# The end of a second attention layer reordered, its loads issued one per step, and 24 products on constants put in front of a mixture of experts

## The reference, cut to what matters

```python
q = (Q @ w_q.T); k = (K @ w_k.T); v = (V @ w_v.T)
attn = softmax(where(causal, einsum('bnghd,bmgd->bnghm', q, k) / sqrt(8), -inf))
x = x + tanh(g_xattn[1]) * (einsum('bnghm,bmgd->bnghd', attn, v).reshape(B, S, D) @ w_o.T + b_o)

z = layernorm(x); logits = z @ w_gate            # 2048 tokens, 8 experts, top 1
mask1 = one_hot(argmax(softmax(logits)), 8)
locations1 = cumsum(mask1, axis=0) - mask1       # place in the expert's queue, capacity 256
mask1 = mask1 * (locations1 < 256)
x = x + tanh(g_ffn[1]) * combine(gelu(dispatched @ w1) @ w2)
```

## Time and profile before

| | before |
|---|---|
| median of 3 executions | 1349.39 us (1348.5 to 1352.16) |
| the profiled execution, its own time | 1351.38 us |
| its span, first to last instruction | 1349.6 us |
| mean granted clock of TensorE | 0.98 of full speed |
| busy: TensorE, VectorE, ScalarE, GpSimd | 93%, 81%, 70%, 52% |
| attention 1: first raw scores to the last residual | from 1031.5 to 1226.7 us of the span |
| experts: first to last product | from 1246.6 to 1343.8 us |

### The profile page before, as it was taken

How to read it: one execution, slowest core, us unless ns; L and a number is a source line. 1 busy time by engine, 2 the same in 40 slices (tenths; PEclk the granted TensorE clock), 3 DMA queues, 4 the chain that set the end, 5 groups by cost and what they waited for, 6 DMA issues and landing times.

```text
span 1349.6 us, 28140 instructions
## 1 busy us (share of the span) xinstructions
PE 1253.2 (93%) x10492; PEld 1091.1 (81%) x10492; DVE 1092.6 (81%) x2203; ACT 946.8 (70%) x2153; POOL 705.6 (52%) x618
## 2 busy tenths in 40 slices
PE   1688999999999999999999999979999999995998
PEld 1577999999999999999999999866776454454998
DVE  8979889999989999989999999986434778765554
ACT  5799877778887778887788887645122466572775
POOL 5657555565665566655655554442000356563575
PEclk9889999999999999999999999999999999996999
DMA  4222332222123222133221010024544324217662
GB/s 146 87 62 69 99 95 87 76 71 65 54 78 88 76 69 68 52 79 89 65 70 35 26 36 24 23 68 140 64 75 72 67 42 74 60 45 242 214 231 80
DMA packets 117574, 110.05 MB, mean 82 GB/s; under 512 B 12187, under 2 KB 101499, under 8 KB 117312
## 3 DMA queue, kind: packets, MB, share of 16 engines
q1 hardware_dynamic: 114320, 99.03, 27.5%
q0 software_dynamic: 2944, 9.19, 1.9%
q10 hardware_dynamic: 176, 0.04, 0.0%
HBM read 80.20 MB, written 28.07 MB: 80 GB/s over the span
## 4 chain that ended last, share of the span: by engine, by line
PE 77%; DVE 14%; issue 3%; ACT 2%; DMA 2%; POOL 1%; POOLq 0%; SPq 0%; ACTq 0%; DVEq 0%
PE PC L577 8%; PE SS L543 7%; PE PO L559 7%; PE B L521 5%; PE PA L479 4%; PE PA L481 4%; PE B L1224 3%; PE PO L1208 2%; PE B L1734 2%; PE SS L535 2%; PE PA L492 2%; PE PA L491 2%; PE PA L493 2%; PE SS L2276 2%; PE PA L504 2%
## 5 line engine op out<-in xcount | busy, mean ns | idle before, releaser
L1021 POOL TENSOR_TENSOR RB<-YS,M 128x512 bf16<-128x512 f32 x128 | 161.3, 1260 | 279.4 <-DVE YS L860 279.4
L665 ACT ACTIVATE QT<-B,sm 128x256 f32<-128x256 f32 x256 | 131.3, 566 | 142.2 <-PE B L521 141.7
L479 PE MATMUL PA<-WH,XQ 128*128 128x256 f32 x512 | 141.0, 307 | 17.9 <-DVE WL L808 13.3
L1016 POOL TENSOR_TENSOR yy<-vv,half 128x14 f32<-128x14 f32 (+1 forms) x64 | 147.6, 2306 | 5.3
L543 PE MATMUL SS<-QT,KT 128*128 128x256 f32 x512 | 133.1, 382 | 7.8 <-DVE mx L812 7.6
L481 PE MATMUL PA<-WL,XQ 128*128 128x256 f32 x512 | 130.1, 286 | 0.0
L824 DVE TENSOR_REDUCE vv<-SQ 128x7 f32<-128x896 f32 (+1 forms) x128 | 120.7, 943 | 0.3 <-ACT SQ L711 0.3
L479 PEld LDWEIGHTS PA<-WH,XQ 128*128 128x128 f32 x512 | 98.9, 193 | 19.1 <-DVE WL L808 13.7
L832 DVE TENSOR_TENSOR QN<-QN,yy 128x512 f32<-128x512 f32 x128 | 114.0, 891 | 0.0
L812 DVE TENSOR_REDUCE mx<-SS 128x4 bf16<-128x512 f32 x128 | 88.0, 687 | 26.2 <-PE SS L535 25.2
L521 PE MATMUL B<-identf,QN 128*128 128x128 f32 x768 | 105.7, 274 | 2.0 <-ACT LNT L620 1.1
(11 more groups left out here) (359 smaller groups left out, 4120.6 us busy)
## 6 DMA issues: line engine op xcount, KB each, us to landing
W<-in_w SPq DMA_DIRECT2D x16, 1024.0 KB
XK<-xk_d SPq DMA_DIRECT2D x24, 512.0 KB, 4.3
V<-v_d SPq DMA_DIRECT2D x112, 64.0 KB
v_d<-VST SPq DMA_DIRECT2D x48, 128.0 KB, 2.0
Q<-qsc SPq DMA_DIRECT2D x48, 128.0 KB
WR<-in_wprojT SPq DMA_DIRECT2D x16, 256.0 KB, 3.0
xk_d<-XK SPq DMA_DIRECT2D x8, 512.0 KB, 3.9
kt_d<-KT SPq DMA_DIRECT2D x64, 64.0 KB, 1.6
```

Source lines behind the costliest of these rows:

```text
L479: pe.matmul(PA[:, 256 * k:256 * k + 256], XQ[:, k, c, bs], wh[:, c, 256 * k:256 * k + 256], start=c == 0, stop=False)
L665: a.activation(QT[i % 2][:, o:o + 256], B1[:, o:o + 256], ACT.Identity, bias=col(n + "b"), scale=col(n + "w"))
L1016: p.tensor_tensor(yy[j % 2][:, :, 0:n], v_, half[:, 0:2 * n].rearrange("p (h k) -> p h k", h=2), ALU.pow).then_inc(s_rstd, 1)
L1021: p.tensor_tensor(RB[i % 2][:], YS[:], M[:], ALU.subtract).then_inc(s_rb, 1)
```

## The change

It has three parts. In attention 1 the 12 loads of the last quarter of queries are issued one per step (steps 33 to 44), each behind a wait for TensorE's progress (`sp_pace`), and the stores of the rows are paced alike and spread over more steps. In the tail the roots are taken block by block (12, 13, 14, 15 apart), the next turns, logits and scales of blocks 8 to 13 come earlier, the choice for the first set stands in step 72 before the normalisation of the last units, and some PSUM banks are exchanged for that; the choice and the address arithmetic have fewer VectorE operations, and the loads of the second and later experts wait for the first gather. Ahead of the first expert TensorE makes 8, 12 and 4 products of a 128x128 identity with 512 columns of ones, into a bank that nobody reads before it is overwritten.

```diff
-        next_bs = [range(0, 4), range(4, 8), range(8, 12), range(12, 15), range(15, 16)]
-        NEXT = {32: 0, 48: 1, 64: 2}
-        LAST = N1 + 11
+        next_bs = [range(0, 4), range(4, 8), range(8, 12), range(12, 13), range(13, 14), range(14, 15), range(15, 16)]
+        NEXT = {32: 0, 48: 1, 63: 2, 67: 3, 71: 4}
+        LAST = N1 + 10
...
+        def sp_pace(sp, n):
+            sp.wait_ge(*((s_S, N + n) if n <= N1 else (s_ST, N + n - 8)))
+        def sp_last_queries(sp, i):
+            half, z = divmod(i, NP)
+            if i == 0:
+                sp.wait_ge(s_qst[3], 32)
+            src = qsc[QPART[z]].rearrange("(a h d) t -> h d a t", h=2, d=8)[half]
+            r0 = 64 * half + 8 * z
+            sp.dma_start(Q6[r0:r0 + 8, 3, :, :], src[:, :, 1536:2048]).then_inc(s_qg[3], 16)
...
-                    if b in (2, 3, 7, 8):
-                        sp_queries(sp, 2 + b // 7, b in (3, 8))
+                    if b in (2, 3):
+                        sp_queries(sp, 2, b - 2)
+                if 33 <= n < 45:
+                    sp_pace(sp, n)
+                    sp_last_queries(sp, n - 33)
...
-                    if 0 <= n - 12 * k - 42 < 12:
-                        sp_next_row(sp, 4 * k + (n - 12 * k - 42) // 3, (n - 12 * k - 42) % 3)
+                    if 0 <= n - 12 * k - 45 < 12:
+                        sp_pace(sp, n)
+                        sp_next_row(sp, 4 * k + (n - 12 * k - 45) // 3, (n - 12 * k - 45) % 3)
+                for p in range(2 * (n - 66), 2 * (n - 66) + 2):
+                    if 0 <= p < 12:
+                        sp_next_row(sp, 8 + p // 3, p % 3)
             sp_load_w(sp, 0)
-            for k in range(2, 5):
-                sp_next_rows(sp, k)
+            for b in range(12, NB):
+                for part in range(3):
+                    sp_next_row(sp, b, part)
...
# pe_attention_1
+                if n == 73:
+                    pe_next_turn(pe, 13)
+                if n == 72:
+                    pe_turn_1(pe, 30)
...
-                if 72 <= n < 76:
-                    pe_logits(pe, n - 64)
+                if 68 <= n < 72:
+                    pe_logits(pe, n - 60)
...
-                if 70 <= n < 74:
-                    pe_next_turn(pe, n - 62)
+                if 66 <= n < 70 or n == 71:
+                    pe_next_turn(pe, n - 58 - (n == 71))
-            pe_logits(pe, 11)
             pe_turn_1(pe, 31)
+            pe_out_proj(pe, 14)
+            pe_logits(pe, 12)
+            pe_out_turn(pe, 15)
+            pe_logits(pe, 13)
             pe_queue_places(pe, 0)
-            pe_out_turn(pe, 15)
             pe_out_proj(pe, 15)
-            for b in (12, 13, 14):
+            for b in (14, 15):
                 pe_next_turn(pe, b)
-            for b in (12, 13, 14):
                 pe_logits(pe, b)
-            pe_next_turn(pe, 15)
-            pe_logits(pe, 15)
...
# dve_attention_1
-                if 67 <= n < 71:
-                    dve_next_scale(v, 2, (n - 59,))
-            dve_logits(v, 10)
-            dve_logits(v, 11)
-            dve_choose(v, 0)
+                if 65 <= n < 69:
+                    dve_next_scale(v, 2, (n - 57,))
+                if n == 69:
+                    dve_next_scale(v, 3, next_bs[3])
+                if n == 72:
+                    dve_next_scale(v, 4, next_bs[4])
+                    dve_logits_quad(v, 2)
+                    dve_choose(v, 0)
+                if n == 73:
+                    dve_normalise(v, 30)
+            dve_normalise(v, 31)
             dve_residual_1(v, 14)
             dve_next_stats(v, 14)
-            dve_next_root(v, 3)
-            dve_normalise(v, 31)
-            dve_next_scale(v, 3, next_bs[3])
+            dve_next_root(v, 5)
             dve_queue_places(v, 0)
+            dve_next_scale(v, 5, next_bs[5])
+            dve_compare(v, range(0, 2))
             dve_residual_1(v, 15)
             dve_next_stats(v, 15)
-            dve_next_root(v, 4)
-            dve_compare(v, range(0, 4))
-            dve_next_scale(v, 4, next_bs[4])
-            dve_compare(v, range(4, 12))
-            for b in range(NB - 4, NB):
-                dve_logits(v, b)
+            dve_next_root(v, 6)
+            dve_compare(v, range(2, 5))
+            dve_next_scale(v, 6, next_bs[6])
+            dve_compare(v, range(5, 12))
+            dve_logits_quad(v, 3)
...
# experts
-        locs = B2[:, 0:128]
+        locs = POa[:, 0:128]
-        who = (B1[:, 0:3 * E], PC[:, 0:3 * E])
+        who = (B1[:, 0:3 * E], B1[:, 3 * E:6 * E])
...
         def sp_experts(sp):
             after_attention_1(sp)
+            sp.wait_ge(s_d[0], 32)
             for x_ in range(1, E):
                 sp_load_w(sp, x_)
...
+        def pe_keep_clock(pe, n):
+            for _ in range(n):
+                pe.matmul(SS[:], identb[:], onesb[:].unsqueeze(1).broadcast_to([128, 4, 128]), start=True, stop=True)
...
             pe_who(pe, 1)
+            pe_keep_clock(pe, 8)
             pe_weights(pe)
+            pe_keep_clock(pe, 12)
             pe_tokens_turn(pe, 0)
+            pe_keep_clock(pe, 4)
...
# dve_choose: the comparison reads the logits themselves; the subtraction moves behind the choice
             v.tensor_reduce(mx, lg, AX, ALU.max).then_inc(*vs.up())
             v.wait_ge(*vs.at())
+            v.tensor_tensor(oh, lg, bc(mx, n), ALU.is_equal).then_inc(*vs.up())
...
-            v.tensor_scalar(oh, lg, 0.0, None, ALU.is_equal).then_inc(*vs.up())
...
# dve_routing: both halves of an expert's list in one operation
-            for z in range(2):
-                w = who[z]
-                v.tensor_copy(TU[:, :, z], w[:, E:2 * E]).then_inc(*vs.up())
-                v.wait_ge(*vs.at())
-                v.scalar_tensor_tensor(out=TI[:, :, z], in0=w[:, 0:E], scalar=128.0, in1=TU[:, :, z], op0=ALU.mult,
-                                       op1=ALU.add).then_inc(*vs.up())
+            v.tensor_copy(TU[:], who_kez[:, 1]).then_inc(*vs.up())
+            v.wait_ge(*vs.at())
+            v.scalar_tensor_tensor(out=TI[:], in0=who_kez[:, 0], scalar=128.0, in1=TU[:], op0=ALU.mult, op1=ALU.add).then_inc(
+                *vs.up())
```

More of the change, by code:

```diff
@@ L1599, in next_bank, with logits_at, turn_bank @@
         def next_bank(b):
-            return PC if b < 8 else (PAh[0], PAh[1], POa, POb)[b % 4]
+            return PC if b < 8 else PAh[b % 2]
+        def logits_at(b):
+            return PC[:, 256:256 + E] if b < 8 else B2[:, E * (b - 8):E * (b - 7)]
+        def turn_bank(u):
+            return {2 * NB - 2: POa, 2 * NB - 1: POb}.get(u, TR[u % 2])
         def every(n, k, first, limit):
@@ L1627, in sp_next_row @@
                 sp.dma_start(out.rearrange("b p h -> p b h")[:, b, :], X[:, b, :]).then_inc(s_out, 16)
[L1629 to L1635, removed]
         def sp_maxima(sp, b):
@@ L1742, in pe_turn_1 @@
                 pe.wait_ge(s_qr, 6)
-            if u % 2 == 0 and b:
+            if b == NB - 1:
+                pe.wait_ge(s_ex, N + N1)
+            elif b and u % 2 == 0:
                 pe.wait_ge(s_oe, b)
-            if u % 2 and b:
+            elif b:
                 pe.wait_ge(s_add, N + b)
@@ L1758, in pe_out_turn @@
                 pe.wait_ge(s_qr, 5 + b)
+            if b == NB - 1:
+                pe.wait_ge(s_oe, b)
             for c in range(2):
@@ L1768, in pe_out_proj @@
                 pe.wait_ge(s_lg, min(b - 4, 8))
+            if b == NB - 1:
+                pe.wait_ge(s_add, N + b)
             for c in range(2):
@@ L1788, in pe_logits @@
             pe.wait_ge(s_xt, b + 1)
+            if b >= 12:
+                pe.wait_ge(s_lg, 12)
             for c in range(2):
-                t = pe.matmul(next_bank(b)[:, 256:256 + E], XF[:, c, 128 * b:128 * b + 128], WG[:, c, :], start=c == 0, stop=c == 1)
+                t = pe.matmul(logits_at(b), XF[:, c, 128 * b:128 * b + 128], WG[:, c, :], start=c == 0, stop=c == 1)
             t.then_inc(s_lgp, 1)
@@ L1938, in act_attention_1 @@
                     act_last_queries_middle(a, (n - 24) // 4)
+            act_next_turn(a, 13)
             act_out_turn(a, 15)
-            for b in (12, 13, 14):
-                act_next_turn(a, b)
+            act_next_turn(a, 14)
+            act_next_turn(a, 15)
             act_split_w1(a, 0, 0)
-            act_next_turn(a, 15)
         def dve_maximum_1(v, i):
@@ L2237, in pe_who @@
                 for z in range(2):
-                    t = pe.matmul(who[z], A[:, b, 128 * z:128 * z + 128], R[:, b].rearrange("p k e -> p (k e)"), start=b == 0,
-                                  stop=b == NB - 1)
+                    t = pe.matmul(who[z], A[:, b, 128 * z:128 * z + 128], R[:, b].rearrange("p k e -> p (k e)"),
+                                  start=b + z == 0, stop=b + z == NB)
             if k:
@@ L2249, in pe_weights @@
                     t = pe.matmul(whose[z], A[:, b, 128 * z:128 * z + 128], RW[:, b].rearrange("p k e -> p (k e)"),
```

(10 more changed lines are left out.)

49 lines of the change are left out of this document (25 added, 24 removed).

## The result

The changed kernel takes 1342.72 us (median of 8 executions, 1340.43 to 1345.08) against 1350.77 for the kernel before beside it (8 executions, 1348.5 to 1360.87). The ratio is 0.9929, 95% interval 0.9908 to 0.9950: some 9.6 us, between 6.8 and 12.4 (the two medians lie 8.0 apart). The forecast was 1338.8 and faster. The profiled execution took 1343.11 us, its span 1341.4.

A forecast was written before the change was run, and what follows sets the result against it. TensorE alone bounds the end from the first expert on, after idle waits on maxima, block 14's residual and the gather. 3.6 + 4.1 + 1.1 + 1.8 = 10.6 us off gives 1338.8 us on the median's scale, range 1334.5 to 1344.

The forecast's parts named there:

- Loads one per step: Attention 1: pacing the last query loads removes TensorE's two waits on the maxima's DMA, 3.6 us, bounds 0 and 3.6.
- Tail: From shifted scores of unit 63 to the addresses: the new order brings these 4.1 us earlier, bounds 1.8 and 5.1.
- the 1.0 set aside: Tail: some twenty uncounted hand-overs at 0.05 us, taken off the 5.1 us gain to leave 4.1.
- Gather and products: Addresses to first expert's first product: faster second gather and transposes in half their time, 1.1 us gained, bounds +1.4 and -1.9.
- rival (d): Second gather no faster without the load beside it: 10.6 - 0.6 = 10.0 us gained, 1339.4; chance 0.06.
- The first expert's clock: First expert's first 24 products at 2.4 GHz if the clock is up: 1.8 us gained, bounds 0 and 1.8.
- the row of 1228 to 1229 us: Clock window: TensorE busy throughout yet still at 1.2 GHz, read as turns and logits of 8 columns.
- the held load: Expert 1's weights, 2.1 MB: 5.5 us plus 2 to land, hidden before ScalarE wants them, 1 us in hand.
- a split of expert 1 waiting for its weights: Expert 1: one of the signs listed as showing the prediction wrong.
- rival (e): Expert 1's load arrives late and TensorE stands still there; slower than before if it takes 19 us; chance 0.04.
- Sum: Whole kernel: 3.6 + 4.1 + 1.1 + 1.8 = 10.6 us gained, 1338.8 us; chance 0.58 as it stands.

The follow-up runs named there:

- paced alone: Kernel before with only the last query quarter's twelve loads issued one per step and row stores of blocks 0 to 7 three steps later; ratio 0.9972, 3.8 us.
- neither: Changed kernel without the held load and without the 24 products on constants; 34.7 us from last raw scores to addresses, against 39.5 with the paced loads alone.

## Why the prediction was right, and where it was not

**Loads one per step**, 3.6: the two waits went, and A fell by 3.8 where nothing else disturbed it. The maxima that the two waits hung on landed in 3.5 and 1.7 us, where 2.1 to 4.2 us of loads were expected in front of them. Not foreseen: the third quarter, still loaded six at a time, leaves a wait of 0 to 1.5 us. Whether the kernel before has it in other executions is open; its profile does not.

**Tail**, 4.1: 4.7 here, 4.8 by the two kernels that differ in it and in the row stores. Behind the last raw scores (1196.6 before, 1194.7 after):

```
                     before  forecast  after
shifted scores 63     15.1     16.4     16.5
first choice          22.3     20.5     20.4
last out projection   27.5     25.2     24.8
residual of block 15  29.6     26.8     26.3
second choice         35.6     31.0     31.4
addresses             39.6     34.5     34.9
```

These steps held within 0.5 us, but two misses cancel in them. Block 15's scale came 0.6 earlier than forecast (28.2 for 28.8). From it to the second choice it took 3.15 us for 2.1, since turn and logits of block 15 ran at 1.2 GHz: the logits, 0.51 in the sum, took 1.02. What the hand-overs took of the 1.0 set aside cannot be told apart from that.

**Gather and products**, 1.1: C fell by 1.6, but little of it by the hold. The second gather took 3.6, 3.6, 3.7 and 5.0 us with it and 3.8 to 5.25 in the ten kernels without; C shows 0.3 for it at most, where 0.6 was forecast, so rival (d) comes near. The rule of the Trainium skill ("DMA: Bandwidth & Descriptors", Queues, rings and completion order), that an engine takes turns between the rows of queues, agrees with what load and gathers did to each other: 12.0 us for 8.7, and some 7 for some 4, neither standing wholly behind the other. How a single engine shared its turns no row shows. What C gained is the transposes and the split at full clock, 0.5, and a gather that came 1.6 sooner than in the one profile before, of which the 12 products left 1.1. That second part is luck: in the three profiles with neither hold nor products C was 10.4, 9.1 and 10.1 ("before", "paced alone", "neither"), as the gather took 5.25, 3.9 or 4.9 us, each time with the load issued before it.

**The first expert's clock**, 1.8: the row of 1228 to 1229 us, which the prediction reads as turns and logits, holds logits alone (line 1790; the turns end at 1227.5). The clock was up, and D without the hold is 1.5 shorter. In the changed kernel D fell by 0.1 only. **The step that failed** is the held load, "hidden, with 1 us in hand": costed at 5.5 + 2 us, it took 12.0, issued beside gathers three and four, which were not in the sum: 0.11 MB moved in its first 3 us, for 0.50 where it ran alone. The prediction's own sign for this, a split of expert 1 waiting for its weights, is in the profile with 2.06 us. That is rival (e), at 1.4 us and not at the 10.6 that would decide.

**Sum**: 3.8 + 4.7 + 1.6 + 0.1 = 10.2 against 10.6, with 1.1 of the gather's scatter in it; the low clock near 1070 us took 1.4 of it in the profiled execution of after. The median lies 3.9 us above the forecast, inside the range; 1.4 of that is the kernel before, which ran at 1350.77 beside it and not at 1349.39. Taking the hold out gives 1.1 by stages; by whole executions the intervals of the two kernels overlap.

## What to carry to other kernels

A load held back from one transfer is issued beside the next ones: put those into its price, and give a late load more slack than its own duration. Work that raises the clock needs work behind it that holds it until the products that count; the half that raises it, alone, lost 2.2 us in the experts, and the half that holds it, alone, 0.4 ahead of them behind a slow gather, an estimated 1.3 behind a usual one. When whole executions scatter by more than the effect, cut the trace at events that both kernels share.

## What the runs showed of the hardware

The granted clock fell for some us near 1070 in half of the profiles, in a stretch that no edit touches, and cost 1.4 us each time. In the tail it fell ahead of block 15's logits in some profiles and behind them in others, also where nothing there was edited: B of one kernel was 34.9 and 34.3. The second 1 MB of a weights load was there 8.2 to 8.8 us after its issue when it went out ahead of four indirect gathers, and 12.0 beside the last two of them. The same gather took 3.6 to 5.25 us in the 14 profiles.
